# A decoder layer on one core: SyncE's stack loads issued ahead of its loads of x and of the residual rows

## The chip, the cores and the metric

One core of a Trainium2 chip runs the whole program in one launch. The metric is the time of one execution on the device, in microseconds (us); three runs are given, with their median, and one more execution was recorded by the hardware profiler. TensorE, VectorE (DVE in the profile), ScalarE (ACT), GpSimd (POOL) and SyncE (SP) each follow an instruction stream of their own and meet on semaphores. Only SyncE issues the plain transfers of this program; it computes nothing.

## The reference

The program is one decoder layer over 32 batches of 256 tokens with 256 features. It is computed in three parts, each followed by a layer norm of its input plus its output:

```python
x = layernorm(x + attn(x, ...))           # 16 heads of 16, rotary, softmax(q k^T / 4) v, out projection
x = layernorm(x + xattn(x, ctx, ...))     # per head two softmaxes over 120 keys: (a1 - lam * a2) v
x = layernorm(x + ffn(x, ...))            # 64 experts, top 6, plus a shared expert, gelu
```

In the first part q and k are rotated by position and the features of a head are paired. In the second each head's 16 features are split into two halves of 8, and each half has its own scores and softmax. All of it is float32. The change lies in the two attention parts; the third part is the same code before and after.

## The kernel before, in words

**Stages and steps.** `attention` does both attention parts, batch by batch, in a software pipeline that is written out by hand. A step works on several batches at once, each at another lag: in a self step X (lag 0) is the batch whose x is loaded, A (1) is projected and split into parts, B (2) has its stacks loaded, its first max scores and its V product made, M (3) has the rest of the max scores, S (4) the scores, exponentials and values, O (5) the output, R (6) the residual with the next bias. A cross step has nearly the same letters, with R for the norm and the gates and Q (7) for the gate weights. Each engine has its own `step` and `cross_step`, generators that `yield` between phases. `run_stage` (L71) unrolls the opening steps and runs the others in a hardware loop over three steps, as the buffers come in threes (`slot`). `run_both` (L86) runs the self steps, then six mixed steps in which the phases of an ending self step and of an opening cross step alternate, then the cross steps. There are 32 batches in each part.

**Parts and stacks.** Float32 products with bf16 operands are made by splitting q and k into three bf16 parts. ScalarE and GpSimd make these in `parts` in turn: for a self batch ScalarE copies the projections with their bias (L1074), GpSimd makes the rotary (L1621 to L1632), ScalarE part 0 (L1118), GpSimd the rest (L1637), ScalarE part 1 (L1131), GpSimd part 2 (L1654). SyncE writes the parts to DRAM (L496, in a cross step L571 and L573) and reads them back in another arrangement: `q_stack` and `k_stack` hold six pairs of parts one under the other, 96 rows for a self batch and two times 48 for a cross batch. For a self batch that takes seven loads (L467), four of q and three of k, 16 to 48 rows of 8 KB each, 1.5 MB in sum. For a cross batch it takes fourteen (L541), 8 to 24 rows each, 1.1 MB in sum. Three slots of the parts in DRAM and three of the stacks are used in turn.

**Who needs the stacks.** TensorE makes max scores from them for batch B in the last two phases of a self step (L613, with the wait at L608) and in the last three of a cross step (L813, wait at L803). VectorE reduces them to the negated maxima (L1324, L1414) and splits those into parts; TensorE transposes them (L752, L1005), ScalarE copies them (L1128, L1298), and SyncE puts them as three more rows on `q_stack` (L485, L554) ahead of the scores (L601, L795) of the next step.

**SyncE's order in a step.** Everything that SyncE issues goes in the order in which the code has it, and a semaphore wait holds all that comes behind it. In a self step before the change:

1. X: wait for the V product of the batch three before (L447), load x, 256 KB (L448).
2. S: wait until the residual slot is free (L454), load the residual rows, 256 KB (L455).
3. B: wait for the parts' landing in DRAM (L459) and for the scores that last used the slot (L462), then the seven stack loads.
4. R: wait for y with the next bias, store it (L471). O: store zeros to two tables (L479).
5. M: wait for the transposed maxima (L483), three loads onto the stack (L485).
6. A: wait for part 2 (L491) and for the slot's last stack loads (L494), write the parts (L496). O: wait for y (L499), store it (L500).

A cross step has the same order: X (x from DRAM, 256 KB, and the context, 120 KB: L517, L518), S (L526), B (waits L529 to L535, loads L541), R (waits and stores of y and of its transpose, L544 to L548), M (L554), Q (L558 to L561), A (L571, L573). In its first steps X also waits for stores of the self part (L507 to L513) and S for the slot's last self use (L522, L523).

**Who needs x and the residual rows.** TensorE uses x one step after its load, in the first phases (L647; in a cross step it transposes it, L886, and uses the context at L855). GpSimd adds a bias to the residual rows one step after their load (L1613), and VectorE adds them to the output (L1378, in a cross step L1581).

Of the kernel before, what the change touches and what calls it, by code (L numbers as in the profile page):

```python
# [15 lines left out]
T = 256  # L16
TC = T // P
FC = DM // P
NH = 16
# [14 lines left out]
def past(b, n):  # L34

    return True if not isinstance(b, int) else b >= n


def opens(a):

    return isinstance(a.n, int) and a.n == 0


def held(eng, count):


    if isinstance(count, int):
        return count
    register = eng.alloc_register()
    eng.reg_mov(register, count)  # L50
    return register
# [50 lines left out]
def attention(nc, n_batches, x_in, xT_in, W, ctxT_in, CW, consts, y_out, res_out, z_out, yT_out, counts_out, moe):  # L102
# [44 lines left out]
    KEYS = ctxT_in.shape[1]  # L147
    E = 2
# [32 lines left out]
    with ExitStack() as ctx:  # L181
# [227 lines left out]
        def _(sp):  # L409
# [31 lines left out]

            def step(at_lag):
                X, A, B, M, S, O, R = (at_lag(lag) for lag in range(7))
                if X.on:

                    if past(X.n, 3):
                        sp.wait_ge(s_vp, X.n - 2)  # L447
                    sp.dma_start(xT[:, X.slot, :, :], xT_rows[X.n]).then_inc(s_x[X.slot], 16)  # L448
                    if opens(X):
                        other_loads()  # L450
                if S.on:

                    if past(S.n, 3):
                        sp.wait_ge(s_sum, S.n - 2)  # L454
                    sp.dma_start(x_res[:, S.slot, :, :], x_rows[S.n]).then_inc(s_res_in[S.slot], 16)  # L455
                if B.on:
                    n_pw = held(sp, 32 * (B.turn + 1))
                    sp.wait_ge(s_init, N_INIT)
                    sp.wait_ge(s_pw[B.slot], n_pw)  # L459

                    if past(B.n, 3):
                        sp.wait_ge(s_sc, NG * (B.n - 2))  # L462
                    q_src = q_dram[B.slot].rearrange("t c (d h) n -> (t c d) (h n)", h=NH)
                    k_src = k_dram[B.slot].rearrange("t c (d h) n -> (t c d) (h n)", h=NH)
                    for is_q, row, src_row, m in STACK_LOADS:
                        stack, src = (q_stack, q_src) if is_q else (k_stack, k_src)
                        sp.dma_start(stack[row:row + m, B.slot, :], src[src_row:src_row + m, :])\  # L467
                          .then_inc(s_st[B.slot], 16)
                if R.on:
                    sp.wait_ge(s_yb, R.n + 1)  # L470
                    sp.dma_start(res_rows[R.n], y_res[:, R.slot, :, :]).then_inc(s_bst[R.slot], 16)  # L471
                    if opens(R):
                        cross_loads()
# [27 lines left out]

            def cross_step(at_lag):
                X, A, B, M, S, R, Q = (at_lag(lag) for lag in (0, 1, 2, 3, 4, 6, 7))
                if X.on:

                    if isinstance(X.n, int) and X.n < C_LAGS:
                        sp.wait_ge(s_stored[X.n % 3], 16 * (X.n // 3 + 1))  # L507
                        if X.n < 3:
                            sp.wait_ge(s_vp, n_batches - 2 + X.n)
                    elif isinstance(X.n, int) and X.n == C_LAGS:  # L510
                        for p in range(3):
                            sp.wait_ge(s_stored[p], 16 * len(range(p, n_batches, 3)))
                            sp.wait_ge(s_bst[p], 16 * len(range(p, n_batches, 3)))  # L513
                    if past(X.n, 3):
                        sp.wait_ge(c_xtp, X.n - 2)
                        sp.wait_ge(c_vp, X.n - 2)
                    sp.dma_start(cx_sb[:, X.slot, :, :], cx_rows[X.n]).then_inc(c_x[X.slot], 16)  # L517
                    sp.dma_start(ctxT[:, X.slot, :, :], ctxT_rows[X.n]).then_inc(c_ctx[X.slot], 16)  # L518
                if S.on:
# [4 lines left out]
                    if past(S.n, 3):  # L524
                        sp.wait_ge(c_sum, S.n - 2)
                    sp.dma_start(x_res[:, S.slot, :, :], cres_rows[S.n]).then_inc(c_res_in[S.slot], 16)  # L526
                if B.on:
                    n_pw = held(sp, 64 * (B.turn + 1))
                    sp.wait_ge(c_wts, 16)  # L529
                    sp.wait_ge(c_pw[B.slot], n_pw)  # L530

                    if not past(B.n, 3):
                        sp.wait_ge(c_ones, B.n + 1)
                    if past(B.n, 3):
                        sp.wait_ge(c_sc, NGR * (B.n - 2))  # L535
                    for e in range(E):
                        q_src = cq_dram[B.slot][e].rearrange("t (d h) n -> (t d) (h n)", h=NH)
                        k_src = ck_dram[B.slot][e].rearrange("t (d h) n -> (t d) (h n)", h=NH)
                        for is_q, row, src_row, m in C_STACK_LOADS:
                            stack, src, n = (q_stack, q_src, T) if is_q else (k_stack, k_src, KEYS)  # L540
                            sp.dma_start(stack[e * HALF + row:e * HALF + row + m, B.slot, 0:NH * n],  # L541
                                         src[src_row:src_row + m, :]).then_inc(c_st[B.slot], 16)
                if R.on:
                    sp.wait_ge(c_y, R.n + 1)  # L544
                    sp.dma_start(cy_rows[R.n][:, :, 0:DM], y_sb[:, R.slot, :, :]).then_inc(c_stored[R.slot], 16)
# [1669 lines left out]
```

## Time and profile before

| What | Value |
|---|---|
| Three runs | 1941.54, 1930.79, 1935.63 us |
| Median | 1935.63 us |
| Profiled execution | 1939.81 us |
| Its span, first to last instruction | 1937.7 us |
| Mean granted TensorE clock | 0.943 |
| TensorE matmul busy | 1695.5 us (87% of the span) |
| VectorE busy | 1310.0 us (68%) |
| ScalarE busy | 1080.8 us (56%) |
| GpSimd busy | 859.0 us (44%) |
| Moved by DMA | 302.86 MB, mean 156 GB/s |

The profiled execution has its own time beside its span; the 2.1 us between them lie around the program's instructions. A time in the rows below is counted from the start of the span. A "busy" matmul is one in flight. An engine's idle time is put down to the instruction or transfer that ended last before it went on. The self steps lie between some 30 and 706 us, the mixed steps between some 690 and 830 us, the cross steps reach to about 1540 us, and the feed-forward part follows.

### The profile page before, as it was taken

The page shows a single profiled execution, that of the slowest core. Times are in us where ns is not written, and L with a number is a line of the kernel's source. Part 1 is how long each engine was busy: PE and PEld are TensorE (multiplying, and loading weights), DVE is VectorE, ACT ScalarE, POOL GpSimd, SP SyncE. Part 2 cuts the span into 40 slices and gives each one's busy share as a digit, 9 for nine tenths or more (in the row PEclk, how much of TensorE's full clock was granted, in tenths as well). Part 3 has the DMA queues.
Part 4 walks back from the last instruction along what each step waited for, and adds up shares of the span by engine and source line. Part 5 has one row for each costly group of instructions (what it writes and reads, how often), then busy time and mean ns, then how long its engine had stood idle before and what let it go on. Part 6 is the DMA issues. An engine that isn't in the chain of part 4 may idle for free. (4 is left out here: it accounts for less than half of the span.)

```text
span 1937.7 us, 43654 instructions
## 1 busy us (share of the span) xinstructions
PE 1695.5 (87%) x14562; PEld 1182.9 (61%) x14562; DVE 1310.0 (68%) x2959; ACT 1080.8 (56%) x1701; POOL 859.0 (44%) x788
## 2 busy tenths in 40 slices
PE   3789999999999997789899999989998669999964
PEld 2566666766666665455555555555555348888853
DVE  3566766777667765679889888878887434443345
ACT  1466666666666665667767777767775311111234
POOL 4567766677767742311211121211210015777565
PEclk7899999999999998899999999999997669999987
DMA  5577866777787775666566666666563146877785
GB/s 121 130 192 181 187 170 168 199 186 183 182 194 186 173 175 137 130 128 128 129 132 137 140 137 138 129 130 130 127 132 68 42 128 173 190 190 188 193 276 194
DMA packets 312887, 302.86 MB, mean 156 GB/s; under 512 B 68850, under 2 KB 289972, under 8 KB 303440
## 3 DMA queue, kind: packets, MB, share of 16 engines
q1 hardware_dynamic: 302544, 288.72, 61.9%
q0 software_dynamic: 10240, 12.81, 3.9%
q8 instruction: 59, 0.97, 0.2%
q14 instruction: 44, 0.36, 0.1%
HBM read 188.42 MB, written 112.00 MB: 155 GB/s over the span
## 5 line engine op out<-in xcount | busy, mean ns | idle before, releaser
L1324 DVE TENSOR_REDUCE att_nmax<-self_p_mx 128x2 f32<-128x512 f32 x512 | 329.0, 687 | 205.5 <-PE self_p_mx L613 205.2
L1414 DVE TENSOR_REDUCE att_cross_nmax<-self_p_mx 128x8 f32<-128x960 f32 x256 | 294.4, 1150 | 77.1 <-PE self_p_mx L813 76.5
L1058 ACT ACTIVATE att_probs<-self_p_sc 128x1024 f32<-128x1024 f32 x256 | 261.0, 1020 | 97.0 <-PE self_p_sc L601 94.9
L1151 ACT ACTIVATE att_probs<-self_p_sc 120x1024 f32<-120x1024 f32 x256 | 261.8, 1023 | 62.0 <-PE self_p_sc L795 61.3
L613 PE MATMUL self_p_mx<-att_k_stack,att_q_stack 96*128 96x256 bf16 x1024 | 161.7, 278 | 56.7 <-DMA att_k_stack<-self_k_parts 51.7
L831 PE MATMUL self_p_pv<-att_probs,att_v_aug 120*32 120x256 f32 x2048 | 169.7, 404 | 0.0
L601 PE MATMUL self_p_sc<-att_q_stack,att_k_stack 99*128 99x256 bf16 x1024 | 158.2, 277 | 11.4 <-ACT att_probs L1058 10.0
L813 PE MATMUL self_p_mx<-att_k_stack,att_q_stack 48*128 48x120 bf16 x2048 | 100.1, 218 | 65.6 <-DVE att_cross_nmax L1414 33.6
L1667 POOL TENSOR_SCALAR att_cross_var_eps<-att_cross_mv 128x2 f32<-128x2 f32 x32 | 7.2, 224 | 330.9 <-DVE att_cross_mv L1520 288.3
L1903 PE MATMUL ffn_p<-ffn_sw,ffn_hT 128*128 128x256 f32 x512 | 127.6, 406 | 28.8 <-ACT ffn_hT L1966 28.4
L613 PEld LDWEIGHTS self_p_mx<-att_k_stack,att_q_stack 96*128 96x128 bf16 x1024 | 96.3, 99 | 85.3 <-DMA att_k_stack<-self_k_parts 37.3
L1681 POOL TENSOR_TENSOR att_qk_rest<-att_qk,att_parts 128x752 f32<-128x752 f32 x32 | 51.7, 1616 | 214.1 <-ACT att_parts L1184 214.1
L628 PE MATMUL self_p_pv<-att_probs,att_v_aug 128*32 128x256 f32 x2048 | 142.3, 397 | 0.5 <-ACT att_probs L1058 0.5
L601 PEld LDWEIGHTS self_p_sc<-att_q_stack,att_k_stack 99*128 99x128 bf16 x1024 | 86.9, 98 | 90.6 <-ACT att_probs L1058 42.6
L813 PEld LDWEIGHTS self_p_mx<-att_k_stack,att_q_stack 48*128 48x128 bf16 x2048 | 66.8, 96 | 108.6 <-DVE att_cross_nmax L1414 66.9
L1912 PE MATMUL ffn_ph<-ffn_xT,ffn_sw 128*128 128x256 f32 x512 | 119.0, 386 | 14.2 <-DMA ffn_x_sb<-x_and_gates 14.2
L1903 PEld LDWEIGHTS ffn_p<-ffn_sw,ffn_hT 128*128 128x128 f32 x512 | 101.8, 204 | 48.2 <-ACT ffn_hT L1966 32.8
L1912 PEld LDWEIGHTS ffn_ph<-ffn_xT,ffn_sw 128*128 128x128 f32 x512 | 97.5, 194 | 27.6 <-issue 14.6
L2089 POOL DMA_INDIRECT expert_sums<-ffn_ye,ffn_slots x64 | 91.9, 1436 | 49.0 <-DMA expert_sums<-ffn_ye,ffn_slots 19.2
L1621 POOL TENSOR_TENSOR att_rope_products<-att_qkb,att_cos_t 128x512 f32<-128x512 f32 x32 | 40.9, 1278 | 154.7 <-ACT att_qkb L1074 154.7
L1966 ACT ACTIVATE ffn_hT<-ffn_ph 128x512 f32<-128x512 f32 x64 | 37.6, 594 | 126.0 <-PE ffn_ph L1912 86.7
L1161 ACT ACTIVATE att_o_raw<-self_p_pv 128x512 f32<-128x512 f32 x128 | 75.8, 592 | 55.9 <-PE self_p_pv L831 55.9
(180 smaller groups left out, 3632.7 us busy)
## 6 DMA issues: line engine op xcount, KB each, us to landing
att_q_stack<-self_q_parts SPq DMA_DIRECT2D x64, 256.0 KB, 5.4
expert_sums<-att_zeros SPq DMA_DIRECT2D x64, 256.0 KB, 8.7
att_q_stack<-cross_q_parts SPq DMA_DIRECT2D x128, 128.0 KB
ffn_w<-in_ffn_w SPq DMA_DIRECT2D x64, 256.0 KB
ffn_m_sb<-expert_sums SPq DMA_DIRECT2D x32, 512.0 KB, 5.5
self_q_parts<-att_parts SPq DMA_DIRECT2D x32, 384.0 KB
self_k_parts<-att_parts SPq DMA_DIRECT2D x32, 384.0 KB
att_k_stack<-self_k_parts SPq DMA_DIRECT2D x32, 384.0 KB, 7.8
```

What stands on the lines that cost most here:

```text
L601: mm = pe.matmul(p_sc[:, w, kc * T:(kc + 1) * T], k_stack[0:RM, S.slot, k_at:k_at + P], q_stack[0:RM, S.slot, u * T:(u + 1) * T], start=Tr ...
L613: mm = pe.matmul(p_mx[:, m % 2, c * T:(c + 1) * T], q_stack[0:RK, M.slot, q_at:q_at + P], k_stack[0:RK, M.slot, m * T:(m + 1) * T], start= ...
L628: mm = pe.matmul(p_pv[j * SLOT:(j + 1) * SLOT, (p % 2) * T:(p % 2 + 1) * T], v_aug[:, S.slot, kc, u, :], probs[:, (u // 2) % 4, (2 * (u % ...
L813: mm = pe.matmul(p_mx[:, e, (2 * hh + c) * KEYS:(2 * hh + c + 1) * KEYS], q_stack[r:r + C_RK, M.slot, q_at:q_at + P], k_stack[r:r + C_RK, ...
L831: mm = pe.matmul(p_pv[j * SLOT:(j + 1) * SLOT, (g % 2) * T:(g % 2 + 1) * T], v_aug[0:KEYS, S.slot, e, 2 * g + hh, :], probs[0:KEYS, g % 4, ...
L1058: act.activation(probs[:, g % 4, :], p_sc[:, :, :].rearrange("p b n -> p (b n)"), ACT.Exp, scale=SCALE).then_inc(s_exp, 1)
L1151: act.activation(probs[0:KEYS, g % 4, :], p_sc[0:KEYS, :, :].rearrange("p b n -> p (b n)"), ACT.Exp, scale=C_SCALE).then_inc(c_exp, 1)
L1324: dve.tensor_reduce(nmax[:, M.slot, :, m], p_mx[:, m % 2, :].rearrange("p (c k) -> p c k", c=TC), AX_X, ALU.max, negate=True).then_inc(s_r ...
L1414: dve.tensor_reduce(cnmax[:, M.slot, :, :, 2 * m:2 * m + 2].rearrange("p c e h -> p e h c"), p_mx[:, :, 0:4 * KEYS].rearrange("p e (x k) - ...
L1903: mm = pe.matmul(p_y[:, tc * DM:(tc + 1) * DM], hT[:, b % 2, k, tc * P:(tc + 1) * P], sw2[:, k, :], start=(k == 0), stop=(k == SK - 1))
L1912: mm = pe.matmul(p_h[:, k // 2, (k % 2) * T:(k % 2 + 1) * T], sw1[:, f, k * P:(k + 1) * P], xT[:, t % 3, f, :], start=(f == 0), stop=(f == ...
L2089: pool.indirect_dma_start(out=moe[j][:, :], out_offset=bass.IndirectOffsetOnAxis(ap=slots[:, e:e + 1], axis=0), in_=ye[:, k % 3, j, :], in ...
```

## The change

In SyncE's `step` and `cross_step` the block of B, with its waits and its loads of the stacks, is moved ahead of the blocks of X and S. In the self step:

```diff
                 X, A, B, M, S, O, R = (at_lag(lag) for lag in range(7))
-                if X.on:
-
-                    if past(X.n, 3):
-                        sp.wait_ge(s_vp, X.n - 2)
-                    sp.dma_start(xT[:, X.slot, :, :], xT_rows[X.n]).then_inc(s_x[X.slot], 16)
-                    if opens(X):
-                        other_loads()
-                if S.on:
-
-                    if past(S.n, 3):
-                        sp.wait_ge(s_sum, S.n - 2)
-                    sp.dma_start(x_res[:, S.slot, :, :], x_rows[S.n]).then_inc(s_res_in[S.slot], 16)
                 if B.on:
                     n_pw = held(sp, 32 * (B.turn + 1))
                     sp.wait_ge(s_init, N_INIT)
                     sp.wait_ge(s_pw[B.slot], n_pw)
...
                         sp.dma_start(stack[row:row + m, B.slot, :], src[src_row:src_row + m, :])\
                           .then_inc(s_st[B.slot], 16)
+                if X.on:
+
+                    if past(X.n, 3):
+                        sp.wait_ge(s_vp, X.n - 2)
+                    sp.dma_start(xT[:, X.slot, :, :], xT_rows[X.n]).then_inc(s_x[X.slot], 16)
+                    if opens(X):
+                        other_loads()
+                if S.on:
+
+                    if past(S.n, 3):
+                        sp.wait_ge(s_sum, S.n - 2)
+                    sp.dma_start(x_res[:, S.slot, :, :], x_rows[S.n]).then_inc(s_res_in[S.slot], 16)
                 if R.on:
```

In the cross step the same is done with its own blocks:

```diff
                 X, A, B, M, S, R, Q = (at_lag(lag) for lag in (0, 1, 2, 3, 4, 6, 7))
+                if B.on:
+                    n_pw = held(sp, 64 * (B.turn + 1))
+                    sp.wait_ge(c_wts, 16)
+                    sp.wait_ge(c_pw[B.slot], n_pw)
+
+                    if not past(B.n, 3):
+                        sp.wait_ge(c_ones, B.n + 1)
+                    if past(B.n, 3):
+                        sp.wait_ge(c_sc, NGR * (B.n - 2))
+                    for e in range(E):
...
                 if X.on:
...
                     sp.dma_start(x_res[:, S.slot, :, :], cres_rows[S.n]).then_inc(c_res_in[S.slot], 16)
-                if B.on:
-                    n_pw = held(sp, 64 * (B.turn + 1))
...
                 if R.on:
```

The new order in a step is B, X, S, R and so on. No instruction of another engine is touched, and SyncE issues the same transfers with the same waits ahead of each.

## Rows read from the trace of the kernel before

**Rows 1.** Busy time by stretch: self steps, cross steps (`us, busy (count) ..., PEclk, DMA share, GB/s`).

```profile
140.00:706.00 566.00, 533.81 (x4536) 384.19 (x4536) 397.03 (x817) 373.99 (x524) 393.38 (x314) 0.99 0.76 184
...
830.00:1430.00 600.00, 553.01 (x6023) 347.85 (x6021) 524.03 (x1195) 438.65 (x733) 119.27 (x156) 0.99 0.63 133
```

**Rows 2.** What TensorE waited for, 140 to 706 us (us, times, longest).

```profile
PE self_p_mx L613 <- DMA att_k_stack<-self_k_parts: 19.4, 20, 3.1
```

**Rows 3.** What TensorE waited for, 830 to 1430 us.

```profile
PE self_p_mx L813 <- DMA att_k_stack<-cross_k_parts: 15.5, 16, 2.9
```

**Rows 4.** SyncE's issues in a self step (start us, us, line, count).

```profile
401.02 0.38 SPq L496 DMA_DIRECT2D self_q_parts<-att_parts  x1
...
403.13 1.07 SPq L448 DMA_DIRECT2D att_xT<-in_x_by_feature  x1
...
405.35 1.72 SPq L467 DMA_DIRECT2D att_q_stack<-self_q_parts  x4
...
418.20 1.79 SPq L485 DMA_DIRECT2D att_q_stack<-att_nmaxT  x3
...
426.57 1.73 SPq L467 DMA_DIRECT2D att_q_stack<-self_q_parts  x4
```

**Rows 5.** TensorE in two self steps (in brackets: idle before, releaser).

```profile
416.93 0.61 PE L613 MATMUL self_p_mx<-att_k_stack,att_q_stack 96*128 96x256 bf16 x4 [0.75 <-DMA att_k_stack<-self_k_parts]
...
422.84 0.61 PE L601 MATMUL self_p_sc<-att_q_stack,att_k_stack 99*128 99x256 bf16 x4
...
438.52 0.61 PE L613 MATMUL self_p_mx<-att_k_stack,att_q_stack 96*128 96x256 bf16 x4 [1.12 <-DMA att_k_stack<-self_k_parts]
```

**Rows 6.** SyncE, a self step without a load of x.

```profile
678.44 0.38 SPq L496 DMA_DIRECT2D self_q_parts<-att_parts  x1
...
682.68 1.71 SPq L467 DMA_DIRECT2D att_q_stack<-self_q_parts  x4
```

**Rows 7.** TensorE, the stacks of that step.

```profile
693.82 0.90 PE L613 MATMUL self_p_mx<-att_k_stack,att_q_stack 96*128 96x256 bf16 x4 [0.31 <-DMA att_k_stack<-self_k_parts]
```

**Rows 8.** Issues from 403 to 409.6 us (count, KB each, median us to landing).

```profile
x_with_bias<-att_y_res SPq DMA_DIRECT2D x1, 256.0 KB, 8.7
att_k_stack<-self_k_parts SPq DMA_DIRECT2D x1, 128.0 KB, 8.8
```

**Rows 9.** SyncE's issues in a cross step.

```profile
1016.10 0.40 SPq L571 DMA_DIRECT2D cross_q_parts<-att_parts  x1
...
1018.90 0.38 SPq L517 DMA_DIRECT2D att_xT<-x  x1
...
1020.81 1.46 SPq L541 DMA_DIRECT2D att_q_stack<-cross_q_parts  x4
```

**Rows 10.** TensorE, the stacks of that step.

```profile
1033.72 0.39 PE L813 MATMUL self_p_mx<-att_k_stack,att_q_stack 48*128 48x120 bf16 x8 [0.39 <-DMA att_k_stack<-cross_k_parts]
```

**Rows 11.** SyncE, a cross step without a load of x.

```profile
1432.82 1.44 SPq L541 DMA_DIRECT2D att_q_stack<-cross_q_parts  x4
```

**Rows 12.** TensorE, the stacks of that step.

```profile
1445.32 0.39 PE L813 MATMUL self_p_mx<-att_k_stack,att_q_stack 48*128 48x120 bf16 x8 [0.86 <-DMA att_k_stack<-cross_k_parts]
```

**Rows 13.** What SyncE waited for, 830 to 1430 us.

```profile
SPq L530 <- DMA cross_k_parts<-att_parts: 10.1, 15, 0.8
```

**Rows 14.** SyncE in a mixed step.

```profile
782.71 0.41 SPq L571 DMA_DIRECT2D cross_q_parts<-att_parts  x1
...
788.71 1.46 SPq L541 DMA_DIRECT2D att_q_stack<-cross_q_parts  x4
```

**Rows 15.** What SyncE waited for, 0 to 230 us.

```profile
SPq L448 <- PE self_p_k L777: 8.3, 2, 6.7
```

**Rows 16.** TensorE before 125 us.

```profile
85.39 1.04 PE L613 MATMUL self_p_mx<-att_k_stack,att_q_stack 96*128 96x256 bf16 x4 [4.42 <-DMA att_k_stack<-self_k_parts]
```

**Rows 17.** Issues from 1018.5 to 1020.6 us.

```profile
att_xT<-x SPq DMA_DIRECT2D x1, 256.0 KB, 3.3
att_x_res<-x_with_bias SPq DMA_DIRECT2D x1, 256.0 KB, 6.0
```

More of the change, by code:

```diff
@@ L503, in cross_step @@
                 X, A, B, M, S, R, Q = (at_lag(lag) for lag in (0, 1, 2, 3, 4, 6, 7))
+                if B.on:
[7 more added lines that the diff above has]
+                    for e in range(E):
+                        q_src = cq_dram[B.slot][e].rearrange("t (d h) n -> (t d) (h n)", h=NH)
+                        k_src = ck_dram[B.slot][e].rearrange("t (d h) n -> (t d) (h n)", h=NH)
+                        for is_q, row, src_row, m in C_STACK_LOADS:
+                            stack, src, n = (q_stack, q_src, T) if is_q else (k_stack, k_src, KEYS)
+                            sp.dma_start(stack[e * HALF + row:e * HALF + row + m, B.slot, 0:NH * n],
+                                         src[src_row:src_row + m, :]).then_inc(c_st[B.slot], 16)
                 if X.on:
@@ L526, in cross_step @@
                     sp.dma_start(x_res[:, S.slot, :, :], cres_rows[S.n]).then_inc(c_res_in[S.slot], 16)
-                if B.on:
-                    n_pw = held(sp, 64 * (B.turn + 1))
[L529 to L542, printed above, removed]
                 if R.on:
```

## The prediction

> **What bounds the kernel now.** I read the busy time by stretch first. TensorE is busy for 533.81 of 566 us in the self steps and for 553.01 of 600 us in the cross steps, at a granted clock of 0.99 of its higher level, while the DMA share is 0.76 and 0.63 [rows 1]. So TensorE comes close to being the bound, and what can be won in the steady steps is the time in which it stands still. The table of waits says for whom: in the self steps the longest sum is the wait ahead of the max scores (L613) for the stacks, 19.4 us in 20 waits [rows 2]; in the cross steps the same wait (L813) costs 15.5 us in 16 waits [rows 3]. These are the transfers that the change puts ahead of others. SyncE's order of issues then shows what stands before them. In one self step the parts go out at 401.02, x is asked for at 403.13, and the stacks from 405.35 on, 4.33 us after the parts [rows 4]. TensorE starts on these stacks at 416.93, 11.58 us after their first load was issued, having stood for 0.75 us, and on the next at 438.52 after 1.12 us [rows 5].
>
> **The start of the loads.** The diff removes and adds no instruction. Two loads (three in a cross step), their two waits and a few register operations go behind seven stack loads (fourteen in a cross step). But the stacks are read back from the parts just written, and SyncE must wait for those to land (L459, L530). How early can that be? In the last step with stacks no x is left to load, so SyncE comes to the wait over 1 us sooner (the issue of x took 1.07 us [rows 4]), and still the stacks start 678.44 to 682.68, 4.24 us after the parts [rows 6]. So in the self steps the start moves forward by 4.33 - 4.24 = 0.1 us, not by the time that the moved issues take.
>
> **The length of the loads.** That same step has only the residual rows ahead, and its stacks are there at 693.82 [rows 7]: 11.14 us after 682.68. The two steps shown give 11.58 (405.35 to 416.93) and 11.95 (426.57 to 438.52) [rows 4, 5], 11.75 in the middle, so x ahead costs 0.6 us. The reason shows in the landings: the last stack load (128 KB) lands 8.8 us after its issue and the store of y_res issued right behind it after 8.7 [rows 8], so the transfers are served nearly in the order of issue, and x and the residual rows are still being served when the first stack bytes could go. Taking the residual rows away too may give as much again or nothing; I take 0.6 for both and 0.1 for the start, 0.7 us, with bounds of 0 and 1.3.
>
> A rule speaks against this. The Trainium skill, DMA: Bandwidth & Descriptors, section "Anatomy of one DMA", gives a fixed cost of about 2.0 us, most of it the receipt after the last byte, and bytes over 436 GB/s on top. By it the two loads, 512 KB or an estimated 1.2 us, fit into the time in which the parts' receipt is outstanding, and the self term would be 0. The step without x [rows 6, 7] speaks against that by 0.6 us.
>
> **What 0.7 us is worth in a self step.** SyncE gets the parts last of a long chain: TensorE projects a batch in the second phase of a step (L647), ScalarE and GpSimd make the rotary and the parts in turn (L1074, L1621 to L1632, L1118, L1637, L1131, L1654), SyncE writes them (L496) and reads the stacks (L467), and TensorE needs them in the seventh phase of its next step. This chain holds two waits for stacks, its own and the one of the batch before. A load that is 0.7 us shorter therefore shortens two steps together by 0.7, one by 0.35. With 566 us at 21.6 us a step (416.93 to 438.52) there are 26 steps: 26 x 0.35 = 9.1 us. The bounds are 0 and the whole 19.4 us.
>
> **The cross steps.** Parts 1016.10, x 1018.90, stacks 1020.81 [rows 9], TensorE at 1033.72 [rows 10]: 4.71 and 12.91 us. With neither x nor the context to load, the stacks issued at 1432.82 [rows 11] are used at 1445.32 [rows 12], after 12.50 us: 0.4 us less. The start can't move much: SyncE already waits for the parts' landing in 15 steps, 10.1 us in sum [rows 13], so I take 0. Here the loop closes in one step (stacks, max scores, the negated maxima's rows at L554, parts, stacks), so all of 0.4 counts, but only where TensorE stands: 16 waits x 0.4 = 6.4 us. The bounds are 0 and 15.5. The moved issues land where SyncE waits for y and x2T anyway (L545, L548), which covers their 1.6 us; without that cover the rows of L554 would be late by as much.
>
> **The mixed steps and the opening.** Where both kinds of step are interleaved, zeros and stores stand between the parts and the stacks: 782.71 to 788.71 [rows 14] is 6.0 us, 1.3 more than 4.71, so the parts have landed and the moved issues are paid in full. There are four such steps with stacks, not all of them with a wait behind; I take 2 us, bounds 0 and 5. In the opening SyncE waits 6.7 us for the V product ahead of a load of x [rows 15], and the second batch's stacks will no longer queue behind that. But the next wait for stacks, 4.42 us ending at 85.39 [rows 16], is set by the third batch's parts, and what is won earlier is waited for there. I take 0, bounds 0 and 4.4.
>
> **The sum.** 9.1 + 6.4 + 2 = 17.5 us. Made against the profiled execution, 1939.81 us (its span of 1937.7 and 2.1 around it), that gives 1922.3; the median of the three runs is 4.2 lower, and 1935.63 - 17.5 = 1918 is the forecast.
>
> **Rivals.**
>
> No gain, 1935. The moved loads were served in time that the stacks could not use. For it: the start is set by the parts' landing, and the difference of 0.4 us in the cross steps is as large as the scatter between steps. Against it: [rows 6, 7]. It also covers a gain that the next wait takes (the transpose of the maxima, L752, needs VectorE's sum with the residual rows, L1378, which runs just ahead of it).
>
> All waits for stacks go, 1900. 19.4 + 15.5 us is 34.9. For it: residual rows count too, and a loop that is no longer late stays so. Against: it needs some 1.5 us in every self step.
>
> Slower, 1962. The moved loads, now issued behind the stacks, are served among them and not after them. One load ahead costs 0.6 us, so two of them in the middle cost 1.2 where 0.6 is paid now: +0.6, halved, in 26 self steps, 8 us; in the cross steps three of them cost 1.2 or less against 0.4 now, some +0.7 in 26 steps (600 us at 23), 18 us; together 26. It decides once more than half of the moved bytes go ahead of the last stack bytes. For it: residual rows issued 1.2 us behind x take 6.0 us to land where x takes 3.3 [rows 17], so order is not strict. Against it: [rows 8]. The same tail would also meet the maxima's rows, issued at 418.20 and needed at 422.84 [rows 4, 5]; those bear a queue that empties up to some 1 us later.
>
> **How the numbers follow.** The forecast's mechanism has 0.55, no gain 0.24, all waits gone 0.10, slower 0.11. A measurement here can tell about 0.5%, 9.7 us. Of the 0.55 I count 0.05 as too small for that. So faster 0.60, same 0.29, slower 0.11. The mechanism's own range is 1905 to 1932; down to all waits gone and up through no gain with the scatter of the runs shown (1930.79 to 1941.54) it becomes 1898 to 1941, which leaves out the slower case and a little below.
>
> **What would show it.** Right: stacks start 4.2 to 4.3 us after the parts in self steps and reach TensorE about 11.1 us later; the sum of waits at L613 in the steady steps falls from 19.4 to about 10 and at L813 from 15.5 to about 9; x lands some 8 us after its issue with nobody waiting at L647 or L886. Wrong: the same 11.75 and 12.9 us (no gain); waits at L613 that grow while x lands in 4 to 5 us (slower); a new wait for the maxima's rows at L601 or L795, or at L752, in place of the old.

## The result and the profile after

The changed kernel took 1970.8 us (median of four runs, 1965.5 to 1976.42) against 1936.62 us for the kernel before (the three runs above and one of 1937.6): 1.0177 times as long, 95% interval 1.015 to 1.0204. It is slower by 34 us, where 18 us less was forecast, and lies outside the range.

The busy time by stretch of the changed kernel, the counterpart of [rows 1]:

```profile
140.00:706.00 566.00, 542.64 (x4598) 388.05 (x4597) 409.51 (x826) 379.37 (x532) 392.43 (x312) 0.99 0.80 185
...
830.00:1430.00 600.00, 530.06 (x5651) 341.76 (x5644) 478.38 (x1129) 419.39 (x696) 114.89 (x150) 0.95 0.75 126
```

In the self steps TensorE is busier than before (542.64 of 566 us for 533.81). In the cross steps it has lost 23 us (530.06 for 553.01), its granted clock is 0.95 for 0.99, and the DMA share is up from 0.63 to 0.75 while fewer bytes move per second. So the same bytes keep the DMA engines busy for longer.

What TensorE waited for in the self steps, the counterpart of [rows 2] (us, times, longest):

```profile
PE self_p_mx L613 <- DMA att_k_stack<-self_k_parts: 10.2, 23, 1.3
...
PE self_p_q L752 <- DVE att_y_sum L1378: 3.2, 3, 2.7
```

and in the cross steps, that of [rows 3]:

```profile
PE self_p_mx L813 <- DMA att_k_stack<-cross_k_parts: 50.9, 24, 3.3
PE self_p_mx L813 <- DVE att_cross_nmax L1414: 11.5, 26, 0.6
```

The second of these lines read so in the kernel before:

```profile
PE self_p_mx L813 <- DVE att_cross_nmax L1414: 20.0, 46, 0.6
```

The wait for the stacks fell from 19.4 to 10.2 us in the self steps, as forecast (about 10), and rose from 15.5 to 50.9 us in the cross steps, where 9 were forecast.

SyncE's timeline in a self step after the change, the counterpart of [rows 4]:

```profile
416.20 0.38 SPq L496 DMA_DIRECT2D self_q_parts<-att_parts  x1
...
420.55 1.72 SPq L455 DMA_DIRECT2D att_q_stack<-self_q_parts  x4
...
423.93 0.41 SPq L461 DMA_DIRECT2D att_xT<-in_x_by_feature  x1
```

and TensorE's on these stacks, that of [rows 5]:

```profile
431.79 0.61 PE L613 MATMUL self_p_mx<-att_k_stack,att_q_stack 96*128 96x256 bf16 x4 [0.53 <-DMA att_k_stack<-self_k_parts]
```

Parts to stacks is 4.35 us and stacks to TensorE 11.24 us, with x now issued 3.4 us behind the first stack load. Before it was 4.33 and 11.58 to 11.95.

SyncE's timeline in a cross step, the counterpart of [rows 9]:

```profile
1015.29 0.39 SPq L571 DMA_DIRECT2D cross_q_parts<-att_parts  x1
...
1019.66 1.43 SPq L518 DMA_DIRECT2D att_q_stack<-cross_q_parts  x4
...
1025.38 0.40 SPq L533 DMA_DIRECT2D att_xT<-x  x1
```

and TensorE's, that of [rows 10]. The third row belongs to the stacks of 1019.66; the first two show what a wait does:

```profile
1009.74 0.39 PE L813 MATMUL self_p_mx<-att_k_stack,att_q_stack 48*128 48x120 bf16 x8 [1.76 <-DMA att_k_stack<-cross_k_parts]
...
1013.47 2.48 PE L1020 MATMUL self_p_q<-att_cross_w_o,att_oT 128*128 128x256 f32 x8
...
1034.33 0.39 PE L813 MATMUL self_p_mx<-att_k_stack,att_q_stack 48*128 48x120 bf16 x8 [2.07 <-DMA att_k_stack<-cross_k_parts]
```

Parts to stacks is 4.37 us (4.71 before), stacks to TensorE is 14.67 us (12.91 before). The output product L1020, 1.99 us long in most steps, takes 2.48 us here. The granted clock in stretches of 1 us shows why (it is the third number from the end, ahead of the DMA share and GB/s):

```profile
1010.00:1011.00 1.00, 1.00 (x17) 0.53 (x12) 0.83 (x1) 0.50 (x1) 0.42 (x1) 1.00 0.89 285
...
1012.00:1013.00 1.00, 1.00 (x18) 0.48 (x14) 0.85 (x3) 0.83 (x2) 0.19 (x1) 0.50 0.07 26
1013.00:1014.00 1.00, 1.00 (x9) 0.50 (x2) 0.99 (x3) 0.51 (x2) 0.00 (x0) 0.50 0.09 22
```

TensorE, just through a wait of 1.76 us, runs at full clock for 1.3 us more and then at 0.50, which is the lower of its two levels. Such stretches add up to 60 us of the 600 in the cross steps after the change and to 12 us before it. After the change there are 15 of them, and each began during a wait for stacks or within 1.9 us behind one. But 7 of the 22 waits of more than 1 us had none. What part of the loss is the clock's, no run separates.

Last, the landings of all 32 issues of a kind (KB each, median us to landing), first in the kernel before:

```profile
att_xT<-in_x_by_feature SPq DMA_DIRECT2D x32, 256.0 KB, 4.1
...
att_xT<-x SPq DMA_DIRECT2D x32, 256.0 KB, 3.8
```

and then in the changed one:

```profile
att_xT<-in_x_by_feature SPq DMA_DIRECT2D x32, 256.0 KB, 8.3
...
att_xT<-x SPq DMA_DIRECT2D x32, 256.0 KB, 9.0
...
x_by_feature<-att_cross_x2T SPq DMA_DIRECT2D x32, 256.0 KB, 8.2
```

x lands 8.3 us after its issue in the self steps and 9.0 in the cross steps, where it took 4.1 and 3.8 before. By that median the x of the cross step above is there at 1034.4, just when its stacks are used (1034.33).

**One measure for all kernels.** For each step with a wait for stacks I took two distances from the timelines of SyncE and TensorE: from the first write of parts to the first stack load (start), and from there to TensorE's first max scores (use). The medians over the steady self steps (300 to 665 us) and cross steps (830 to 1430 us), and the mean period between first stack loads:

| Kernel | self start, use, period | cross start, use, period | cross parts to use |
|---|---|---|---|
| before | 4.35, 11.67, 21.26 | 4.79, 12.66, 22.92 | 17.45 |
| changed | 4.35, 11.11, 21.13 | 4.38, 14.23, 24.41 | 18.61 |

Use can be read only where TensorE waits, which are the late steps: 16 of 26 cross steps before, 23 of 24 after. So the table makes the kernel before look later than it is. The trace also has each increment that a load adds to its semaphore. The last increment of a batch's stack loads is their landing, and it can be read in every step. From the first stack load to it the median is 11.50 us before and 10.98 after in the self steps, and 12.09 before and 14.10 after in the cross steps. By this measure the cross stacks are 2.0 us late, and not 1.6.

### The profile page after: what moved, and what is told of

It reads as the page before. It is cut to its first block and busy times, and to the rows that moved or that the text cites. A ratio compares the mean times of both kernels' runs of the same rounds, so it can differ in the third digit from the quotient of the medians.

```text
span 1963.4 us, 43654 instructions
## 1 busy us (share of the span) xinstructions
PE 1704.6 (87%) x14562; PEld 1195.9 (61%) x14562; DVE 1299.9 (66%) x2959; ACT 1086.4 (55%) x1701; POOL 860.1 (44%) x788
## 5 line engine op out<-in xcount | busy, mean ns | idle before, releaser
L831 PE MATMUL self_p_pv<-att_probs,att_v_aug 120*32 120x256 f32 x2048 | 177.7, 421 | 0.0
L813 PEld LDWEIGHTS self_p_mx<-att_k_stack,att_q_stack 48*128 48x128 bf16 x2048 | 74.3, 99 | 121.9 <-issue 53.0
L1681 POOL TENSOR_TENSOR att_qk_rest<-att_qk,att_parts 128x752 f32<-128x752 f32 x32 | 51.8, 1618 | 212.7 <-ACT att_parts L1184 212.7
L795 PE MATMUL self_p_sc<-att_q_stack,att_k_stack 51*128 51x256 bf16 x1024 | 105.9, 287 | 2.4 <-ACT att_probs L1151 2.4
```

The source lines that it names most:

```text
L795: mm = pe.matmul(p_sc[:, e, hh * T:(hh + 1) * T], k_stack[r:r + C_RM, S.slot, h * KEYS:h * KEYS + P], q_stack[r:r + C_RM, S.slot, h * T:(h ...
L813: mm = pe.matmul(p_mx[:, e, (2 * hh + c) * KEYS:(2 * hh + c + 1) * KEYS], q_stack[r:r + C_RK, M.slot, q_at:q_at + P], k_stack[r:r + C_RK, ...
L831: mm = pe.matmul(p_pv[j * SLOT:(j + 1) * SLOT, (g % 2) * T:(g % 2 + 1) * T], v_aug[0:KEYS, S.slot, e, 2 * g + hh, :], probs[0:KEYS, g % 4, ...
```

## The experiments

The theory after the result: in the cross steps the moved loads are in flight beside the stack loads and slow them, while in the self steps they queue up behind. The rivals: the self steps' new order spoils the later steps; having nothing ahead of the stacks is what slows them; one kind of load does the harm. The kernels below start from the kernel before, except the two under "Behind the stacks' landing", even_after and even_all_after: these start from the changed kernel and have the new order in the self steps too. Ratios are to the kernel before, run at the same time; its medians were 1930.25 us for the first four kernels, 1933.58 for the next four, 1932.72 for even_before, even_after and res_in_eights, and 1936.27 for even_all_after. A kernel "in one run" has its time and its distances from a single execution.

### One half at a time

The edit is the change's own, in `step` alone or in `cross_step` alone.

> The stacks go first in the self steps alone; the cross steps keep the order of before. Theory (the loss is made in the cross steps, by the moved loads that are served among the stack loads): the self steps keep what they won, stacks used 11.1 us after their first issue, and the whole comes out 7 to 12 us below before, ratio near 0.995; waits at L813 between 830 and 1430 us stay near 15 us. Rival (the self steps' new order leaves the later steps in a worse rhythm): L813 waits near 50 us and a time above before.

Measured: 0.9978 of before (0.995 to 1.0006), 1929.66 us. Self steps: start 4.36, use 11.10, period 21.13; cross steps: 4.83, 12.60, 23.00. The wait in the cross steps:

```profile
PE self_p_mx L813 <- DMA att_k_stack<-cross_k_parts: 24.8, 20, 2.5
```

> The stacks go first in the cross steps alone. Theory: stacks start 4.4 us after the parts in place of 4.8, but are used 14.2 us after their first issue in place of 12.4; period near 24.3 us against 22.6; 35 to 45 us above before, ratio near 1.020. Rival (the loss needs the self steps' new order too): within 10 us of before.

Measured: 1.0166 (1.0106 to 1.0226), 1961.9 us, 32 us above before where 35 to 45 were expected. Cross steps: start 4.17, use 14.07, landing 13.95, period 24.10:

```profile
PE self_p_mx L813 <- DMA att_k_stack<-cross_k_parts: 55.2, 24, 4.5
```

The loss sits in the cross steps alone. The gain of the self steps is real in the distances but too small for the time to tell from none. The 24.8 us of waits here against 15.5 before, with the same cross code, is the size by which such a sum differs between two executions.

### Which load

The blocks of a cross step in SyncE's code, in their order:

```text
before:            X, S, B, R
cross_res_behind:  X, B, S, R
cross_x_behind:    S, B, X, R
```

> In the cross steps the load of the residual rows (256 KB) alone goes behind the stacks; x and the context stay ahead. Theory (bytes behind the stacks are served among them and slow them in proportion): 256 of the 632 KB cost 256/632 of the 1.85 us, so stacks used some 13.1 us after their first issue, time 5 to 20 us above before. Rival A (having nothing ahead of the stacks is what slows them): 12.4 us as before, since x and the context are still ahead. Rival B (one kind of load does the harm, and it is this one): 14 us.

Measured: start 4.76, use 13.34, landing 13.26, period 23.82; 1964.17 us in one run.

```profile
PE self_p_mx L813 <- DMA att_k_stack<-cross_k_parts: 40.0, 22, 3.4
```

> In the cross steps x and the context (376 KB in two loads) go behind the stacks, the residual rows stay ahead. Theory (in proportion to bytes): stacks used some 13.5 us after their first issue, time 10 to 30 us above before. Rival A (nothing ahead is what slows them): 12.4 us. Rival B (one kind of load does the harm): 14 us here and 12.4 with the residual rows behind, or the reverse.

Measured: start 4.64, use 13.95, landing 13.84, period 24.29; 1976.68 us in one run.

```profile
PE self_p_mx L813 <- DMA att_k_stack<-cross_k_parts: 52.3, 24, 3.8
```

Use is 12.66 us with none of the loads behind, 13.34 with 256 KB, 13.95 with 376 KB and 14.07 to 14.23 with all 632 KB. The landings say the same: 12.09, 13.26, 13.84, and 13.95 to 14.10 us. The delay grows with what is behind, either load does it, and something ahead of the stacks doesn't protect them. Both rivals fall. The times ran higher than I had expected of such parts of the change (5 to 20 and 10 to 30 us), as high as for the whole: the period had already reached 23.8 and 24.3 us.

### Behind the stacks' landing

Against the changed kernel, the stores of y and x2T move up to just behind the stack loads, and a wait follows them:

```diff
+                if R.on:
...
+                    sp.dma_start(yT_out[R.n], x2T[:, R.slot, :, :]).then_inc(c_tst[R.slot], 16)
+                if B.on:
+                    n_st = held(sp, 16 * C_N_ST * (B.turn + 1))
+                    sp.wait_ge(c_wts, 16)
+                    sp.wait_ge(c_st[B.slot], n_st)
                 if X.on:
...
```

> The changed kernel, but in a cross step SyncE issues the stores of y and x2T right behind the stacks, then waits until the stacks have landed, and only then issues x, the context and the residual rows. Theory (moved loads in flight beside the stacks slow them): the stacks start 4.4 us after the parts and are used no later than before, 12.0 to 12.6 us after their first issue in place of 14.2; period in the cross steps 22.0 to 22.6 us; 1910 to 1930 us, at or up to 1% below before. Rival (nothing ahead of the stacks, or their earlier start, is what slows them): still 14 us and 1960 or more. Rival (x or the context comes too late when it is issued at the end): new waits of TensorE at L886 or L855.

Measured: 0.9955 (0.9937 to 0.9973), 1925.89 us. Cross steps: start 4.25, use 13.05, landing 12.90, period 22.96. SyncE's waits, of which the first two are the new one:

```profile
SPq L529 <- DMA att_k_stack<-cross_k_parts: 55.8, 14, 5.4
SPq L542 <- DMA att_k_stack<-cross_k_parts: 44.6, 12, 4.9
...
SPq L558 <- ACT att_cross_nmaxT L1302: 17.6, 24, 2.2
```

With the moved loads still behind the stacks but no longer in flight beside them, the loss of 1.8% is gone. The cross steps are back at the level of before and not ahead of it: 25 of them take 576.8 us for 575.2, and use and period missed what was expected (12.0 to 12.6 and 22.0 to 22.6). What the whole kernel wins lies in the self and mixed steps. That SyncE stands for 100 us more there costs nothing, since the next thing it is wanted for (L558, the maxima's rows) is still waited for. No wait of TensorE for x or the context appears.

> As cross_behind_landed, with the two stores of y and x2T behind the wait too, so that nothing is in flight beside the stacks. Theory (any transfer beside them slows them, stores as well as loads): stacks used 11 to 12 us after their first issue, 0.5 to 1 us sooner than with the stores beside them. Rival (only loads into SBUF do it): as in cross_behind_landed. Time within 10 us of that kernel, as TensorE is near its bound, or somewhat above it if the stores and loads still run when the maxima's rows or the parts are due.

Here R goes behind the wait too. Measured: 1.0058 (1.0038 to 1.0078), 1944.46 us. Cross steps: start 4.28, use 12.96, landing 12.84, period 23.79:

```profile
PE self_p_mx L817 <- DMA att_k_stack<-cross_k_parts: 37.7, 22, 3.7
...
PE self_p_sc L799 <- DMA att_q_stack<-att_cross_nmaxT: 3.3, 9, 0.8
```

With nothing at all beside them the stacks still take 12.96 us, 0.1 less than with the two stores beside them, not the 0.5 to 1 expected. That is an answer to a question I had not asked: alone, they can be in use 4.28 + 12.96 = 17.24 us after the parts, and before the change, in its late steps, they were after 17.45. Over all steps start and landing add up to 17.12 us alone and to 16.89 before. So the loads ahead of the stacks cost them nothing that this test can show, and in the cross steps there was nothing to win by moving them. The kernel is slower, as I read it, because SyncE's five issues now stand right ahead of the maxima's rows, in the loop: from use to the next parts it takes 23.79 - 17.24 = 6.55 us in place of 5.47, and TensorE has a new wait at L799.

### Even and uneven rows

Why are the self steps spared? Their stack loads have 16, 32 and 48 rows; those of the cross steps have 8, 16 and 24. The first test makes the self steps uneven.

```diff
-            STACK_LOADS.append((is_q, at * HD, part_of[at] * HD, n_run * HD))
+            step_rows = 8 if n_run == 1 else n_run * HD
+            for r0 in range(0, n_run * HD, step_rows):
+                STACK_LOADS.append((is_q, at * HD + r0, part_of[at] * HD + r0, step_rows))
```

> Order of before; in the self steps the three stack loads of 16 rows are each made as two of 8 rows (10 loads in place of 7, same bytes). Theory (the cross stacks suffer since loads of 8 and 24 rows leave some of the 16 DMA engines with less to do, which go on to the transfers behind): by itself this costs issue time and balance, stacks used 12 to 14 us after their first issue in place of 11.7.

Measured: self steps: start 4.34, use 13.41, landing 13.16, period 22.65; 1976.32 us in one run. TensorE's wait from 300 to 665 us:

```profile
PE self_p_mx L615 <- DMA att_k_stack<-self_k_parts: 27.0, 15, 2.9
```

> The same split of the self stack loads, with the stacks first in the self steps (cross steps as before). Theory (unbalanced stack loads let what is behind them run among them): the gain of 0.6 us that the new order had with balanced loads is gone or turns into a loss against self_split_before. Rival (balance has nothing to do with it; the loss in the cross steps comes from x's rows being read from DRAM tables that the kernel wrote, or from the number of loads): the new order is still 0.5 us or more better than self_split_before.

Measured: self steps: start 4.35, use 14.52, landing 14.40, period 23.90; 1997.62 us in one run.

```profile
PE self_p_mx L615 <- DMA att_k_stack<-self_k_parts: 37.1, 16, 3.9
```

Ten loads of the same bytes, some of 8 rows, take 1.7 us longer than seven; whether by their number or their rows, this pair of kernels can't tell. And the new order, which made the even loads 0.56 us faster (11.67 to 11.11), makes the uneven ones 1.1 us slower (13.41 to 14.52). The sign turned with how the loads are cut, in the same steps, with the same x and residual rows behind.

The second test makes the cross steps even. The six pairs of parts and their places in the buffer are permuted, so that all runs are two parts long: twelve loads of 16 rows in place of fourteen.

```diff
+    C_PAIRS = [(1, 0), (0, 2), (1, 1), (0, 0), (0, 1), (2, 0)]
+    PLACE = (1, 0, 2)
...
-        part_of = [pair[0 if is_q else 1] for pair in PAIRS]
+        part_of = [PLACE[pair[0 if is_q else 1]] for pair in C_PAIRS]
...
-                act.activation(cparts[:, 0, :], cqk[:, :], ACT.Copy).then_inc(c_hi, 1)
+                act.activation(cparts[:, PLACE[0], :], cqk[:, :], ACT.Copy).then_inc(c_hi, 1)
```

(and so for the other uses of `cparts` by part, L1188, L1681, L1685).

> Order of before; the cross batches' pairs of parts and the places of the parts are permuted so that the same stack rows come in 12 loads of 16 rows, in place of 14 of 8, 16 and 24 rows. Same bytes, same products. Theory (a load's rows are dealt out over as many of the 16 DMA engines as divide them, and the fullest engine sets the end): per cross batch the fullest engine has 6 rows of 8 KB and 6 of 3.75 KB, 72 KB in place of 95, so the stacks are used 10 to 11 us after their first issue in place of 12.6, waits at L813 nearly vanish, 8 to 20 us below before. Rival (number of bytes or of issues alone counts): 12 us or more, within 5 us of before.

Measured: 0.9944 (0.9923 to 0.9964), 1920.79 us. Cross steps: start 4.87, period 22.68; TensorE waited in 2 of 26 steps only, so use can't be read; the stacks land 10.29 us after their first issue (10 to 11 was expected).

```profile
PE self_p_mx L815 <- DVE att_cross_nmax L1416: 29.8, 82, 0.6
...
PE self_p_mx L815 <- DMA att_k_stack<-cross_k_parts: 1.7, 2, 1.3
```

> Order of the changed kernel with the same 16-row loads in the cross steps. Theory (uneven stack loads are what lets the moved loads run beside them; with even loads the order of issue holds on every engine): stacks used up to 0.6 us sooner than in even_before, as in the self steps, the loss of the change is gone, 1905 to 1925 us. Rival (the loss comes from x, context or residual rows being behind at all): stacks used 1.5 us later than in even_before, and the time 15 us or more above it.

Measured: 0.9914 (0.989 to 0.9937), 1915.53 us, 5 us below even_before. Cross steps: start 4.26, landing 10.62, period 22.67, one wait of 0.3 us, after 11.69 us.

```profile
PE self_p_mx L815 <- DVE att_cross_nmax L1416: 30.4, 86, 0.6
...
PE self_p_mx L815 <- DMA att_k_stack<-cross_k_parts: 0.3, 1, 0.3
```

A cross step of it in SyncE's timeline:

```profile
1004.38 0.51 SPq L575 DMA_DIRECT2D cross_k_parts<-att_parts  x1
1006.95 1.25 SPq L520 DMA_DIRECT2D att_q_stack<-cross_q_parts  x3
...
1011.02 1.36 SPq L520 DMA_DIRECT2D att_k_stack<-cross_k_parts  x3
1012.72 0.41 SPq L535 DMA_DIRECT2D att_xT<-x  x1
```

The landing of x in its cross steps:

```profile
att_xT<-x SPq DMA_DIRECT2D x26, 256.0 KB, 5.6
```

x is issued 5.8 us behind the first stack load, as in the changed kernel, and lands after 5.6 us, not 9.0. The loss of the change is gone. The time alone wouldn't prove that the order of service holds here, since these stacks land 1.8 us sooner than the uneven ones and a delay could hide in that slack. The landings settle it: 10.29 us before and 10.62 after, 0.3 us more where the uneven loads had 2.0 more, while the start came 0.6 sooner. The expected 0.6 us less didn't come, and the periods are the same (22.68 and 22.67), as are the 25 cross steps (568.8 and 569.0 us). So the 5 us between the two kernels don't come from the cross steps; the order of the self steps differs too.

The four cases side by side, landing in us after the first stack load:

| Stack loads | increments per batch | moved loads ahead | moved loads behind |
|---|---|---|---|
| self, 7 of 16 to 48 rows | 112 | 11.50 | 10.98 |
| cross, 12 of 16 rows | 192 | 10.29 | 10.62 |
| self, 10, six of them of 8 rows | 118 | 13.16 | 14.40 |
| cross, 14 of 8, 16 and 24 rows | 176 | 12.09 | 14.10 |

Counted from the first write of the parts, with the start added, the new order brings the landing 0.5 and 0.3 us forward in the first two rows and puts it back by 1.2 and 1.6 us in the last two. The number of loads can't be what turns the sign: ten with some of 8 rows lose, twelve of 16 rows don't. The second column counts the increments that the trace records on the stacks' semaphore. A load of 16 rows or a multiple of it adds 16. The others add fewer: 9 for 8 rows and 13 for 24 rows give 118 and 176 exactly.

One more test of the same kind was less clear.

```diff
-                    sp.dma_start(x_res[:, S.slot, :, :], cres_rows[S.n]).then_inc(c_res_in[S.slot], 16)
+                    for r in range(0, P, 8):
+                        sp.dma_start(x_res[r:r + 8, S.slot, :, :], cres_rows[S.n][r:r + 8, :, :])\
+                          .then_inc(c_res_in[S.slot], 16)
```

> As cross_res_behind (in the cross steps the residual rows behind the stacks, x and context ahead), but the 256 KB of residual rows are made as 16 loads of 8 rows, which is 16 KB each. Theory (such loads go to the same DMA engines as the uneven stack rows and queue behind them in order): stacks used 12.4 to 12.8 us after their first issue, no later than before, against 13.3 when the residual rows are one load. Rival (bytes in flight slow the stacks wherever they run): 13.3 us or more.

Measured: start 4.75, use 12.83, landing 12.72, period 23.17; 1942.91 us in one run.

```profile
PE self_p_mx L815 <- DMA att_k_stack<-cross_k_parts: 29.2, 21, 2.6
```

Each of the sixteen loads adds 9 increments. Use is 12.83 us where one load of 128 rows gave 13.34 and none behind gave 12.66, just above the 12.4 to 12.8 us of the theory and well below the rival's 13.3. But the landing, 12.72, is still 0.6 us above the 12.09 of before, and sixteen issues also push the two stores 5 to 7 us back, behind the landing. So it counts as support only.

### The same in the self steps

```diff
-    PAIRS = [(0, 0), (0, 1), (0, 2), (1, 0), (1, 1), (2, 0)]
+    PAIRS = [(1, 0), (0, 2), (1, 1), (0, 0), (0, 1), (2, 0)]
+    PLACE = (1, 0, 2)
...
```

> even_after with the same permutation in the self steps: six stack loads of 32 rows in place of seven of 16, 32 and 48. The bytes per DMA engine are 96 KB as they were. Theory (the fullest engine's bytes set the end): the stacks are used 11.0 us after their first issue as in even_after, and the time is within 5 us of it, 1910 to 1920 us. Rival (the number of loads counts too): 0.4 us sooner for the one load less, waits at L613 from 6 us to nearly 0, and 3 to 5 us below even_after.

Measured: 0.9851 (0.9817 to 0.9885), 1905.44 us. In the steady self steps no wait for stacks is left; TensorE's longest waits are these:

```profile
PE self_p_q L754 <- DVE att_y_sum L1380: 5.9, 17, 0.4
PE self_p_sc L603 <- ACT att_probs L1060: 4.1, 17, 0.2
```

The period there is 21.14 us, as in even_after (21.12), so in the steady steps the end of the waits for stacks brought no time: others, such as the one at L754, took their place. But the theory behind the expectation, that the fullest engine's bytes set the end, failed: the stacks land 9.23 us after their first issue where even_after has 10.94, with the same bytes and 16 increments per load in both. That is 1.7 us sooner, where the two expectations were 0 and 0.4. Against even_after the profile is 8 us ahead at the tenth V product (237.9 us for 245.9) and a little over 10 at the first output product of the cross steps (809.6 for 820.4), in the opening and the mixed steps, where TensorE waits most. So the number of loads, or the new arrangement of the pairs that comes with it, counts more than either expectation gave it; no run separates the two. The same holds for even_before: its 1.8 us sooner landing came with 16-row loads, with two loads fewer and with another arrangement, and which of them gave it is not shown. The cross steps of this kernel:

```profile
830.00:1430.00 600.00, 555.15 (x6057) 344.67 (x6053) 539.67 (x1223) 441.45 (x738) 121.59 (x159) 1.00 0.68 134
```

## Why the prediction was wrong

**The step that failed** is the term of the cross steps, 16 waits x 0.4 = 6.4 us gained, and under it the premise that "the transfers are served nearly in the order of issue", so that the loads put behind the stacks would leave them alone. I had seen one landing that matched an orderly queue, and it was of a self step [rows 8]. I carried it over to the cross steps, where the stack loads have other row counts. Measured, 25 cross steps (from the fourth output product to the twenty-ninth) take 609.3 us in place of 575.2, +34.1 us.

**Point by point:**

- *Start, self* (0.1 us forward): 0.0, 4.35 in both. The landing of the parts sets it.
- *Length, self* (0.6 us less): 11.67 to 11.11, 0.56 less. The step without a load of x [rows 6, 7] had told this rightly. The fixed cost of 2.0 us that the Trainium skill gives (DMA: Bandwidth & Descriptors, "Anatomy of one DMA") would have hidden the two loads. That section fits it to transfers issued by GpSimd, and these are SyncE's; the runs show a little more than half a microsecond that was not hidden.
- *Worth per self step* (half of it, 0.35): from the tenth to the last V product the five kernels with the new self order and the old cut of the self loads take 469.4 us on average (468.3 to 469.8), the six with the old order 475.5 (473.0 to 478.4). That is 6.1 us in 22 steps, 0.28 in each, which is half of 0.56. At 26 steps it would be 7.2 us, where 9.1 were predicted: the halving was right and the 0.7 a little too large. The whole kernel self_only, 0.9978 (0.995 to 1.0006), can't tell such a gain from none.
- *Opening* (0): the fifth V product comes 4.6 us sooner, and at the tenth nothing is left of it (245.2 us on average with the new order, 244.9 with the old). The next waits took it back, as argued.
- *Start, cross* (0): 4.79 to 4.38, 0.4 us sooner. SyncE did come to its wait a little late in some steps.
- *Length, cross* (0.4 us less): use 1.57 us later, landing 2.0. The one control that I had, 12.50 against 12.91 [rows 10 to 12], was within the scatter of single steps; the rival of no gain said so, and the kernel with nothing beside the stacks showed no gain to be had (17.12 us from parts to landing, 16.89 before).
- *Mixed steps* (2 us gained): from the last V product to the fourth output product 178.8 us for 175.4, 3 us lost. self_only has 176.9 and cross_only 180.9, so the cross order is what lost them; that it did so in the same way is argued, not measured.
- *Bound of the cross steps* (all 15.5 us of waits): too generous as well. With the waits down to 1.7 us (even_before) the 25 cross steps still take 568.8 us, 6.4 less, while the waits for VectorE's reduction rise from 20.0 to 29.8. What one wait gives back the next takes.

**The rival that came true** is the slower one. It had the mechanism in a cross step right and the size too small: +0.7 us a step, where the distance from parts to use grew by 1.2, that from parts to landing by 1.6, and the period by 1.5. Its 1962 was 9 us short. It was wrong for the self steps, where order held. Its condition was misplaced too: x lands some 14.6 us after the first stack load, when the stacks have landed (14.1) and not well before them, and still slows them. The question to ask was which of the DMA engines a load can use. The Trainium skill states it (DMA: Bandwidth & Descriptors, "Why a DMA increments its semaphore by 16 and not by 1"): a transfer is spread over the largest number of engines up to 16 that divides its outer counts, and on SyncE's queue over the lowest-numbered. By that a load of 8 rows uses 8 engines and one of 24 uses 12, and the others go on to what is issued next. The runs agree in sign and place (self_split, even), and so do the increments: 16 for loads of 16, 32 and 48 rows, 9 for 8 rows and 13 for 24, which is one more than the 8 and 12 of that rule. Which engines the increments come from the trace doesn't tell, so that the others went on to what follows isn't seen directly.

**What stays open:** what the stack loads share with the loads that run beside them. If each engine keeps to its order, an engine full of stack rows isn't held up by its own queue, and something common to the engines must be what slows it; that is argued, not shown. The trace's single packets show that both sides are slowed. In the cross steps a packet of 1 KB, which is a row of x, of the residual rows or of a store, takes 61 ns on average before and 95 after the change, but 59 in cross_behind_landed and 66 in even_after. One of 8 KB, a row of the q stack, takes 767 ns before and 872 after. But it takes 852 with nothing beside the stacks too, so these rows also slow each other. No run here tells whether it is the reading of DRAM, the ways into SBUF or the making of descriptors.

## What to carry to other kernels

Before moving a transfer behind one that matters, look at how the one that matters is cut: if its row counts leave DMA engines idle (here loads of 8 and 24 rows, with 9 and 13 increments for 16), what follows may run beside it and not behind it. Cutting the loads into 16 rows and multiples was worth at least as much here as any order: 0.9944 (0.9923 to 0.9964) alone, where the best order with the old cut had 0.9955 (0.9937 to 0.9973), 0.9914 with the new order, 0.9851 with six loads of 32 rows in the self steps too. And check a control of one stage in that stage; a landing read in the self steps says nothing about the cross steps.

## What the runs showed of the hardware that was not expected

- The same 1.5 MB of stacks in ten loads, six of them of 8 rows, landed 13.16 us after the first issue, in seven loads of 16 to 48 rows after 11.50 us (moved loads ahead in both), and in six loads of 32 rows after 9.23, where seven in that order had 10.94.
- A higher DMA share is no sign of a higher rate: in the cross steps of the changed kernel it rose from 0.63 to 0.75 with 126 GB/s in place of 133, and in even_all_after it is 0.68 with 134.
- A wait of 1.76 us was followed, 1.3 us later, by a stretch at the lower clock, and the mean granted clock of the cross steps fell from 0.99 to 0.95 when waits of 2 to 3 us became the rule, though none was longer than 3.3 us and 7 of 22 had no such stretch behind them. With the waits gone it is 1.00.
